# Attention of a two-layer block: four passes over two head couples each, as a loop of three passes and one pass in straight code, or as four passes in straight code

## What is computed

```python
xd = (x @ W_down).reshape(b, t, h, s)                      # 16 heads of 16
keys = einsum('bthk,hik->bthi', xd, tokeys) * scale
queries = einsum('bthk,hik->bthi', xd, toqueries) * scale
values = einsum('bthk,hik->bthi', xd, tovalues)
dot = einsum('bqhs,bkhs->bhqk', queries, keys)
attn = softmax(dot, axis=-1)
out = einsum('bhqk,bkhs->bqhs', attn, values).reshape(b, t, e)
return out @ W_unify + b_unify
```

## Time and profile before

| what | value |
|---|---|
| median of 3 runs | 3974.03 us (3969.38 to 3999.69) |
| the profiled execution, its own time | 3956.84 us |
| its span, first to last instruction | 3955.0 us |
| mean granted TensorE clock | 0.972 |
| PE busy | 3784.0 us, 96% |
| DVE busy | 3306.2 us, 84% |
| ACT busy | 2727.7 us, 69% |
| POOL busy | 453.2 us, 11% |
| instruction fetch (queues q8, q14) | 258 and 141 packets, 4.23 and 1.16 MB |

### The profile page before, as it was taken

One profiled execution on the slowest core, in us unless ns is written; L12 is line 12 of the kernel. 1 busy time (PEld: TensorE's weight loads), 2 busy tenths in 40 slices (PEclk: granted clock), 3 DMA queues, 4 the chain that ended last, 5 costly groups with the idle time before them and its releaser, 6 DMA issues. The chain is left out here.

```text
span 3955.0 us, 84753 instructions
## 1 busy us (share of the span) xinstructions
PE 3784.0 (96%) x31366; PEld 1957.8 (50%) x31366; DVE 3306.2 (84%) x3515; ACT 2727.7 (69%) x4939; POOL 453.2 (11%) x402
## 2 busy tenths in 40 slices
PE   8799899999999999999999999999997859999998
PEld 6587333333333333333333333333334538888887
DVE  6567799999899999989999999999973837766664
ACT  2454688888788888878888888888885422223332
POOL 0133200000000000000000000000002225002323
PEclk9899999999999999989999999999998979999999
DMA  4811331122022122112202112201113011005332
GB/s 140 234 28 22 105 36 21 12 26 28 11 25 33 10 23 26 20 14 25 29 9 31 29 10 26 33 10 7 10 31 83 1 52 59 1 2 148 77 78 38
DMA packets 301759, 158.58 MB, mean 40 GB/s; under 512 B 218397, under 2 KB 273507, under 8 KB 298800
## 3 DMA queue, kind: packets, MB, share of 16 engines
q1 hardware_dynamic: 289072, 142.49, 18.9%
q0 software_dynamic: 12288, 10.70, 1.6%
HBM read 86.46 MB, written 64.18 MB: 38 GB/s over the span
## 5 line engine op out<-in xcount | busy, mean ns | idle before, releaser
L1210 ACT ACTIVATE probs<-attention_scores_t_sums 128x512 f32<-128x512 f32 x4096 | 2217.3, 597 | 313.6 <-PE attention_scores_t_sums L1134 96.9
L1244 DVE TENSOR_REDUCE max_parts<-attention_scores_q_sums 128x1 f32<-128x1024 f32 x1008 | 1223.8, 1222 | 53.2 <-PE attention_scores_q_sums L1128 46.3
L1244 DVE TENSOR_REDUCE attention_max_parts<-attention_scores_q_sums 128x1 f32<-128x1024 f32 x992 | 1207.4, 1224 | 16.7 <-PE attention_scores_q_sums L1128 9.2
L1134 PE MATMUL attention_scores_t_sums<-q_operand,k_operand 50*128 50x512 f32 x2048 | 767.3, 454 | 14.3 <-ACTq L1224 14.0
L1134 PE MATMUL attention_scores_t_sums<-attention_q_operand,attention_k_operand 50*128 50x512 f32 x2048 | 751.3, 445 | 0.0
L1128 PE MATMUL attention_scores_q_sums<-attention_k_operand,attention_q_operand 48*128 48x512 f32 x2048 | 745.1, 443 | 0.0
L1128 PE MATMUL attention_scores_q_sums<-k_operand,q_operand 48*128 48x512 f32 x1952 | 726.2, 452 | 5.2 <-issue 5.2
L1143 PE MATMUL attention_o_psum_sums<-probs,v_heads 128*32 128x256 f32 x8192 | 667.4, 398 | 2.0 <-ACT o_parts L1206 0.2
L1143 PE MATMUL attention_o_psum_sums<-probs,attention_v_heads 128*32 128x256 f32 x8208 | 655.8, 391 | 1.9
L1128 PEld LDWEIGHTS attention_scores_q_sums<-attention_k_operand,attention_q_operand 48*128 48x128 f32 x2048 | 301.4, 184 | 421.8 <-DVE attention_max_parts L1244 188.6
L1128 PEld LDWEIGHTS attention_scores_q_sums<-k_operand,q_operand 48*128 48x128 f32 x1952 | 293.7, 188 | 421.3 <-DVE attention_max_parts L1244 177.1
(11 more groups left out here) (322 smaller groups left out, 4620.7 us busy)
## 6 DMA issues: line engine op xcount, KB each, us to landing
o_other_half<-o_parts SPq DMA_DIRECT2D x130, 64.0 KB, 2.0
expert_rows<-attention_empty_rows SPq DMA_DIRECT2D x16, 516.0 KB, 5.7
v_scratch<-value_chunk SPq DMA_DIRECT2D x16, 512.0 KB, 4.9
w_whole<-in_L_ffn_ew SPq DMA_DIRECT2D x8, 1024.0 KB, 6.9
experts_w_whole<-in_L_ffn_ew SPq DMA_DIRECT2D x8, 1024.0 KB, 5.7
q_operand<-q_scratch SPq DMA_DIRECT2D x24, 256.0 KB, 4.9
k_operand<-k_scratch SPq DMA_DIRECT2D x24, 256.0 KB, 6.5
attention_q_operand<-q_scratch SPq DMA_DIRECT2D x24, 256.0 KB, 4.8
```

The lines of the kernel that those rows point to most:

```text
L1134: nc.tensor.matmul(ST[bank_n][:, :], KOP[b][64 * h:64 * h + ROWS + 2, kt * P:(kt + 1) * P], QOP[b][64 * h:64 * h + ROWS + 2, c * CH:(c + 1 ...
L1210: nc.scalar.activation(PR[:, tile, :], ST[bank_n][:, :], ACT.Exp).then_inc(st_free, 1)
L1244: nc.vector.tensor_reduce(MPART[par][:, h, u // 4, u % 4:u % 4 + 1], SA[h][:, :], AX.X, ALU.max)\
```

## The change

`halves` no longer makes a loop: it calls `body` four times with `i` a plain number, and the five callers no longer pass their engine. The bodies are not touched, so every engine's instructions for passes 1 to 3 now stand written out, each with constants, as those of pass 4 did. Lines behind it move up by 2 (1128 is now 1126, and so on).

```diff
-        def halves(engine, body):
-
-            with engine.Fori(0, NP // 2 - 1) as i:
-                body(i, False)
-            body(NP // 2 - 1, True)
+        def halves(body):
+            for i in range(NP // 2):
+                body(i, i == NP // 2 - 1)
...
-            halves(sp, body)
+            halves(body)
...
-            halves(pool, body)
+            halves(body)
...
-            halves(pe, body)
+            halves(body)
...
-            halves(act, body)
+            halves(body)
...
-            halves(dve, body)
+            halves(body)
```

## The result

| what | before | changed |
|---|---|---|
| median of 10 runs each, taken side by side | 3979.64 us | 3963.48 us |
| lowest to highest | 3969.38 to 3999.69 | 3958.11 to 3972.51 |
| ratio of changed to before, 95% interval | | 0.996 (0.9945 to 0.9974) |
| the profiled execution's own time | 3956.84 | 3962.38 |

The changed kernel is 0.4% faster, 16.2 us of median. The forecast was 0.8% (30.5 us). The sign, the range and the likeliest of the three cases (within 1%) came out, and the size was nearly twice too large. One oddity comes first: the profiled execution of the changed kernel is no faster than that of the kernel before. Both facts need an explanation.

What follows compares the result with a forecast made beforehand. DVE was taken to set each round, with PE's pause and slow clock lost at two pass borders. Terms -34.6 + 1.0 + 3.1 = -30.5 us took the 3974.0 us median to 3943.5 us, 0.8% faster, range 3924 to 3968.

Steps and rivals of the forecast that it cites:

- the likeliest of the three cases: Whole kernel: time within 1% of the kernel before, chance 0.73, against 0.24 for faster and 0.03 for slower.
- The bound and the mechanism: Attention: DVE sets a round; at the first two borders PE pauses for its jump, then runs at half clock.
- Step 1: First two pass borders: without the jumps back, pause and clock fall both go, gaining 34.6 us; lower bound 5.2 us.
- Step 2: First two borders: they still lose 0.50 us each on a shared score bank, as the third does; 1.0 us back.
- Step 3: 48 rounds of passes 1 to 3: straight form takes 39.735 against 39.67 us a round, 3.1 us slower.
- Rival a: First two borders: slow clock belongs to the profiled execution, only pauses are won, -1.1 us, 3973; chance 0.12.
- The branch rule: Loop's jumps back: a taken branch out of the resident blocks waits for its target's DMA fetch; 3.6 us on PE.
- Steps 4 and 5: Passes 1 to 3: removed register instructions (107 us of ACT's sequencer) gain nothing; more distinct code adds no fetches.
- rivals c, d and e: Border loss not the jump's, 3977, 0.03; straight code's fetch runs dry, 4030, 0.03; register instructions on the path, 3890, 0.02.
- The offset of 17.2 us: Whole kernel: the shown median, 3974.0 us, stood 17.2 above the profiled execution; the forecast kept the same difference.
- rival b: First two borders: they cost more in timed runs, so the 17.2 us go too, -47.7 us, 3926; chance 0.12.

Runs made afterwards that it cites:

- pause kernels: Changed kernel with TensorE made to wait at the first two borders for one, two or three small SyncE DMAs: 3932.01 us, 3943.69 us, no median read.
- the other chip: Both kernels run again unchanged on another chip: the kernel before 3947.01 us, the changed one 3929.04 us, ratio 0.9955.

## Why the prediction was off, step by step

**The bound and the mechanism** were right. DVE sets the round, the borders lose by a pause and then by the clock, and taking the jumps away leaves none of either. The pause kernels show both halves apart: 1.28 us of pause costs 0.9 us more than the changed kernel's border, and 2.41 us costs 7.2 and 7.6 us more, of which some 5.9 (13.7 x 0.43) are the clock's.

**Step 1 (gain 34.6 us) is the step that failed, by its size.** Its sum was right for the execution it was read from. Its words "I take all of it" went from one execution to the median, and four executions of that same program lose 34.6, 15.4, 33.8 and 19.9 us. By the medians, with steps 2 and 3 as the traces have them, the term is 16.2 + 1.0 + 3.1 = 20.3 us, and 16.7 + 1.0 + 3.1 = 20.8 on the other chip (3945.74 - 3929.04 = 16.7). The mean of the four traces is 25.9, with single values from 15 to 35, so it does not contradict this and can't fix it closer. What was too large in the 34.6 is the clock's part: the pauses were 2.60 us there and 2.3 to 2.9 in all. The lower bound of the step, 5.2 us for the pauses alone, was sound and not reached: at all eight borders of the loop the clock did fall.

**Rival a had the right idea and the wrong form.** It asked whether the clock falls in every run, all or nothing, and gave the alternative -1.1 us. What varies is how long it stays down. A rival "it falls everywhere, but half as long" would have kept the pauses (5.2 us) and halved the rest of the 34.6: -(5.2 + 29.4 / 2) + 1.0 + 3.1 = -15.8 us, close to the 16.2 measured. The evidence against rival a, two borders with the same 0.82, looked like agreement and was chance.

**The branch rule.** The Trainium skill, "Runtime: NRT & Kernel Launch", section "Instruction fetch mechanics", lets a taken branch wait for its target's fetch. The runs agree for PE, DVE and ACT: DVE's next instruction comes 2.9 us after its branch, though the branch's record says 63 ns. Around the first jump of the kernel before, from 1064 to 1072 us, the instruction queues q8 and q14 move 7 packets; at the same border of the changed kernel, from 1060 to 1068, they move one. That fits a fetch, though no row ties a packet to the engine that waits. The prediction saw the jump on PE alone and took DVE's to cost nothing. That did not touch its sum, since the change takes all jumps away; freeing PE alone buys nothing, as the runs showed.

**Step 2 (1.0 us back)** was right: 40.17 and 40.23 us at the borders, and 39.72 once the bank changes over them.

**Step 3 (3.1 us back)** was right in size: the rounds of passes 1 to 3 are 39.72 to 39.75. Its reason was open, with ACT's register folding and phase as the guess. It is the order of the two waits of one copy a round, 0.05 to 0.06 us; the exponentials' own waits, exchanged, left the round at 39.72.

**Steps 4 and 5 (nothing)** held. The changed kernel moves 3.92 MB of instructions by q8 instead of 4.23, and no pause by "issue" stands in its attention; rivals c, d and e fell with that.

**The offset of 17.2 us** between the profiled execution and the median was carried over without a cause. The runs take it apart. The measurement with the median of 3974.03 lies some 34 us above later ones for both kernels, jumps or not. The profiled execution, 3956.84 us, is itself 11 us above the 3945.74 that the kernel before takes later, since its borders lost so much. So the one part (34 us) stays in the changed kernel, and rival b, which wanted the offset to go with the jumps, fell; and the other is the fault of step 1 seen from the other side. That the forecast of 3943.5 us lies 20 us below the 3963.48 measured comes from both: 14 us are step 1's, and 5.6 that the median before was 3974.03 by three runs and 3979.64 by ten.

**Not settled:** what decides whether the clock falls (1.28 us of idle time without a fall, 1.33 us with one), why the slow stretch behind a pause lasts from 3.4 to 44 us, and whether it is longer behind a jump (eight borders, mean 24 us) than behind a wait for a DMA (four, 13.7, 13.7, 6.8, 3.4); where TensorE had no jump but waited for the jumping engines it was 23.9 and 27.3. Nor which jump costs the kernel with only TensorE straight its gain (ACT's is the likeliest), nor what slowed the gated block in one trace and made all runs of that measurement some 34 us longer.

## What to carry to other kernels

A stall's cost that includes a fall of TensorE's clock is a draw. Before pricing it, take it from several executions. The timed runs' own clocks help: with the price of slow time (here 0.43 us for each us at half clock) their spread tells without a further trace how much of a kernel's scatter is the clock, though not at which place. When a loop's back edge is removed, look at every engine: here freeing TensorE alone won nothing and leaving TensorE alone in the loop lost everything, while VectorE alone in the loop cost some 0.5 us a border. Where an instruction on the path has two constant waits, try the one that ends last first in the source, and compare the idle time in front of the instruction by hundredths: 0.29 against 0.23 us at one copy was the whole difference between two forms of a round, and the same exchange at an exponential won nothing.

## What the runs showed of the hardware

- TensorE's clock after a pause. With one pause of 1.28 us it fell at neither border of its trace, with one of 1.33 or 1.44 us it fell at both, and with 2.3 to 3.6 us at 13 of 14, though PE had work for nearly all of the time around it (82.03 of 85.75 us in the worst window shown). It then stayed at 1.2 GHz for 3.4 to 44 us, without relation to the pause's length (3.57 us of pause and 6.8 us of low clock; 2.44 and 44.4).
- The record of a taken branch may hold the delay behind it (PE, 3.6 us) or not (DVE, 63 ns, with the next instruction 2.9 us later). The gap to the engine's next instruction is what counts.
- All five engines jumping together hold PE no longer than its own jump alone (2.3 to 2.9 us against 2.38 and 2.79).
- Of two constant waits on one ScalarE copy one is carried by an instruction in front (17 ns). With the wait that ends last on the copy itself, it starts 0.23 us after PE instead of 0.29.
- An engine's jump need not cost what it stalls: DVE idle for 1.86 us by "issue" held PE for 0.93 us and cost the border 0.6.
